# Vision tower with routed experts on one core: softmax scaling on VectorE, biases by matmul, an order of stages for each engine

## What is computed

```python
h = tok(x)                                   # patch projection with shifted images, layer norm
h = h + attn_rope(norm(h))                   # 8 heads, rope; two layer norms; relu net 128-512-128 (x1, net, x2)
h = h + mix(norm(h))                         # triangular W1, gelu, triangular W2, with biases b1, b2
h = h + dif(norm(h))                         # two softmax maps a1 - lam*a2, group norm over features, out_w, out_b
x = norm(h); x1 = ln(x)                      # "moe": attention, then the router
x = x + attn(x1) @ wo
x2 = ln(x)
gate, e = top_2(softmax(x2 @ wr))            # 64 experts, capacity 72 rows each
pos = rank of the (token, choice) in its expert; kept if pos < 72
buf[e, pos] = x2
y = gelu(buf @ w1[e] + b1[e]) @ w2[e] + b2[e]
h = h + x + sum over 2 choices of gate * y[e, pos]
```

## Time and profile before

| what | value |
|---|---|
| median of 3 runs (lowest, highest) | 435.94 us (434.51, 436.28) |
| the profiled execution's own time | 436.75 us |
| its span in the profile | 435.0 us |
| busy: PE / PEld | 311.8 us (72%) / 275.6 us (63%) |
| busy: DVE / ACT / POOL | 229.7 (53%) / 219.0 (50%) / 250.5 us (58%) |
| mean TensorE clock granted | 0.823 of full speed |
| DMA | 50.07 MB |

### The profile page before, as it was taken

How to read it: one execution, slowest core, us unless ns; L and a number is a source line. 1 busy time by engine, 2 the same in 40 slices (tenths; PEclk the granted TensorE clock), 3 DMA queues, 4 the chain that set the end, 5 groups by cost and what they waited for, 6 DMA issues and landing times.

```text
span 435.0 us, 10303 instructions
## 1 busy us (share of the span) xinstructions
PE 311.8 (72%) x3840; PEld 275.6 (63%) x3840; DVE 229.7 (53%) x642; ACT 219.0 (50%) x635; POOL 250.5 (58%) x382
## 2 busy tenths in 40 slices
PE   1886668779775776748785357323999999999960
PEld 0563557677544565736675256212999999999960
DVE  1145585872549999898857763911222323223224
ACT  0133646777478875586676224300255555555530
POOL 5046684778877534374657758778055555555560
PEclk9896869999966977976886558555599999999995
DMA  8999900000000000000000100003888999999406
GB/s 258 425 394 285 124 2 2 3 2 2 1 2 2 2 2 2 3 2 2 2 2 2 27 2 15 6 8 69 159 257 308 306 326 312 324 317 312 163 10 163
DMA packets 25818, 50.07 MB, mean 115 GB/s; under 512 B 4100, under 2 KB 16012, under 8 KB 25642
## 3 DMA queue, kind: packets, MB, share of 16 engines
q1 hardware_dynamic: 22730, 46.91, 35.0%
q0 software_dynamic: 3040, 2.52, 2.0%
HBM read 43.92 MB, written 7.72 MB: 119 GB/s over the span
## 4 chain that ended last, share of the span: by engine, by line
PE 33%; DVE 8%; POOL 4%; ACT 4%; issue 3%; DMA 1%; POOLq 0%; DVEq 0%; SPq 0%
PE bank L705 18%; PE scores L705 13%; ACT work L979 3%; POOL slot_rows L640 2%; DVE work L1207 1%; DVE mx L1197 1%; PE bank L771 1%; PE bank L929 1%; DMA ring<-expert_rows 1%; DVE work L1233 1%; ACT norm L979 1%; DVE norm L1380 1%; DMA expert_rows<-work,put_u 0%; DVE norm L1381 0%; DVE top_i L1299 0%
## 5 line engine op out<-in xcount | busy, mean ns | idle before, releaser
L979 ACT ACTIVATE work<-scores,b1T 128x72 f32<-128x72 f32 x256 | 61.1, 321 | 77.8 <-PE scores L705 77.8
L705 PE MATMUL bank<-ring,work 128*72 128x128 f32 x512 | 98.6, 277 | 0.0
L697 POOL DMA_INDIRECT expert_rows<-work,put_u x64 | 59.9, 936 | 59.7 <-issue 39.5
L705 PE MATMUL scores<-work,ring 128*128 128x72 f32 x512 | 92.2, 265 | 0.0
L705 PEld LDWEIGHTS scores<-work,ring 128*128 128x128 f32 x512 | 80.2, 199 | 0.0
L1369 DVE TENSOR_SCALAR work<-bank,work 72x128 f32<-72x128 f32 x64 | 22.2, 347 | 78.6 <-PE bank L705 78.6
L979 ACT ACTIVATE work<-bank 128x288 f32<-128x288 f32 (+3 forms) x136 | 46.4, 374 | 31.2 <-PE bank L705 25.3
L705 PEld LDWEIGHTS bank<-ring,work 128*72 128x72 f32 x512 | 54.7, 147 | 0.2 <-ACT work L979 0.2
L674 POOL TENSOR_TENSOR work<-work,sm 100x288 f32<-100x288 f32 x32 | 26.0, 834 | 21.3 <-DVE sm L1223 16.4
L979 ACT ACTIVATE work<-work 100x1152 f32<-100x1152 f32 (+1 forms) x20 | 20.4, 1018 | 31.3 <-DVE work L1207 29.6
L705 PE MATMUL bank<-wT,xTp 128*128 128x128 f32 x192 | 33.6, 349 | 1.4 <-ACT work L979 1.4
(11 more groups left out here) (153 smaller groups left out, 614.9 us busy)
## 6 DMA issues: line engine op xcount, KB each, us to landing
ring<-in_experts SPq DMA_DIRECT2D x64, 512.0 KB, 4.9
work<-in_patches SPq DMA_DIRECT2D x4, 864.0 KB, 12.2
slot_rows<-blank SPq DMA_DIRECT2D x1, 2340.0 KB, 30.0
work<-slot_rows SPq DMA_DIRECT2D x7, 292.5 KB
wT<-in_weights SPq DMA_DIRECT2D x1, 1664.0 KB, 17.7
expert_rows<-mid POOLq DMA_DIRECT2D x2, 576.0 KB, 9.3
ring<-expert_rows SPq DMA_DIRECT2D x4, 288.0 KB, 4.6
expert_rows<-work,put_u POOLq DMA_INDIRECT x64, 4.3
```

Of the source, the lines that this page charges most:

```text
L697: pool.indirect_dma_start(out=ytok[:, :], out_offset=bass.IndirectOffsetOnAxis(ap=put_u[:, e:e + 1], axis=0), in_=ys[0:CAP, e % NY, :], in ...
L705: return nc.tensor.matmul(o, a, b, start=start, stop=stop)
L979: return nc.scalar.activation(o, i, f, **kw)
```

## The change

1. The table `ORDER_FOUND` becomes `ORDERS_FOUND` with an own order of the 252 remaining stages for each of the four engines.
2. Softmax scaling: POOL's half (L674) is gone. DVE scales all four quads with one instruction, and `dif_mix` is one instruction instead of four.
3. `mix_base` and `dif_base` are gone. PE puts the bias row into the bank first (`biased`: a matmul with one row of ones, 96 x 384 out), and the output matmuls add to it. The constants grow by 96 columns.
4. `rt_norm_b` on ACT writes straight into `xrow`, without g and b; after `rt_turn` ACT copies the row to its second place (`rows_doubled`). POOL's L627 and L631 are gone. DVE applies g and b per feature when it takes the transposed slot rows to SBUF (`x_in_place`). Since `xrow` has two buffers, ACT waits in `rt_norm_b` of batches 2 and 3 for the scatters of batches 0 and 1.
5. `rt_store` leaves the order: POOL does the four additions after all router stages, before the first expert's scatter.
6. `x1_affine` has two operations instead of three; be1 and b2 are added once.
7. `blank`, the source of the first fill of `slot_rows`, lies in the tile `hid`; ACT waits for that DMA before the first `net_in`.

```diff
-ORDER_FOUND = """
-    tok_z:0 tok_shift:0 tok_z:1 tok_turn:0 tok_norm_a:0 tok_z:2 tok_norm_b:0 tok_shift:1 tok_turn:1 tok_z:3
...
+ORDERS_FOUND = {
+    "pe": """
+    tok_z:0 tok_shift:0 tok_z:1 tok_shift:1 tok_turn:0 tok_z:2 tok_turn:1 tok_shift:2 tok_norm_a:0 tok_z:3
...
-    return [tuple((w.split(":")[0], int(w.split(":")[1]))) for w in ORDER_FOUND.split()]
+    return [tuple((w.split(":")[0], int(w.split(":")[1]))) for w in ORDERS_FOUND[engine].split()]
...
-                if stage in ("mix_base", "dif_base"):
-
-                    pool.wait_ge(S["var"], var_of[name + "_norm_a", b])
-                    pool.tensor_tensor(tiles(mid, b), tiles(h, b), row("L0_ffn_b2" if stage[0] == "m" else "L1_attn_out_b"), ALU.add
-                                       ).then_inc(S["base_ready"], 1)
...
                 if stage == "rt_count":
 
-                    pool.wait_ge(S["normed"], normed_count["rt", b])
                     t = slice(TPB * b, TPB * b + TPB)
-                    st.link(pool.tensor_tensor(tiles(mid, b), tiles(norm, b), row("L1_ffn_ln2_g"), ALU.mult))
                     if b >= 2:
                         pool.wait_ge(slots_sent[b - 2], 16 * 2 * TPB)
-                    st.step(pool.tensor_copy(xrow[:, b % 2, :, :, D], const("ids", TP).rearrange("p (n k) -> p n k", k=2)[:, t, :]))
-                    st.link(pool.tensor_tensor(xrow[:, b % 2, :, :, 0:D], tiles(mid, b).unsqueeze(2).broadcast_to([TP, TPB, 2, D]),
-                                               row("L1_ffn_ln2_b").unsqueeze(2).broadcast_to([TP, TPB, 2, D]), ALU.add))
+                    st.link(pool.tensor_copy(xrow[:, b % 2, :, :, D], const("ids", TP).rearrange("p (n k) -> p n k", k=2)[:, t, :]))
+                    pool.wait_ge(S["rows_doubled"], b + 1)
...
-                if stage in ("rope_sums", "moe_sums", "dif_sums", "dif_sums2"):
...
-                    for q in range(QUADS // 2):
...
-                        last = pool.tensor_tensor(
-                            to, e3, sm[:, s, 2 * PAIRS * q:2 * PAIRS * (q + 1)].unsqueeze(2).broadcast_to([SROWS, 2 * PAIRS, SEQ]), ALU.mult)
...
+            for b in range(NB):
+                pool.wait_ge(S["out_added"], out_count["moe_out", b])
+                pool.tensor_tensor(tiles(h, b), tiles(h, b), tiles(src, b), ALU.add).then_inc(S["h_summed"], 1)
...
+            def biased(job, name):
+
+                o = fill(pe, job)
+                pe.wait_ge(S["rows_in"], 16)
+                mm(o[0:TP, 0:TPB * D], const("ones")[0:1, :], rows[0:1, ROWS.index(name), :].unsqueeze(1).broadcast_to([1, TPB, D]),
+                   start=True, stop=False)
...
+                    if name == "rt" and b >= 2:
+                        act.wait_ge(slots_sent[b - 2], 16 * 2 * TPB)
...
+                    if stage == "rt_turn":
+                        act.wait_ge(S["normed"], normed_count["rt", b])
+                        go(xrow[:, b % 2, :, 1, 0:D], xrow[:, b % 2, :, 0, 0:D]).then_inc(S["rows_doubled"], 1)
...
-                    for q in range(QUADS // 2, QUADS):
...
-                    last.then_inc(S["half_scaled"], 1)
+                    to = e4 if stage[:3] == "dif" else probs[0:SROWS, f % 2, :, :, :, 0:SEQ].rearrange("p q a b k -> p q (a b) k")
+                    v.tensor_tensor(to, e4, s3.unsqueeze(3).broadcast_to([SROWS, QUADS, 2 * PAIRS, SEQ]), ALU.mult
+                                    ).then_inc(S["map_scaled" if stage[:3] == "dif" else "probs_ready"], 1)
...
-                v.tensor_copy(xe[:, e % NX, :], banks[i][:, 0:CAP]).then_inc(S["xe_ready"], 1)
+                v.tensor_scalar(xe[:, e % NX, :], banks[i][:, 0:CAP], col("L1_ffn_ln2_g"), col("L1_ffn_ln2_b"), ALU.mult, ALU.add
+                                ).then_inc(S["xe_ready"], 1)
```

215 lines of the change are left out of this document (142 added, 73 removed).

## The result

The changed kernel took **427.83 us** (median of 4, 427.35 to 428.91), the kernel before 435.23 us beside it (434.21 to 436.28): ratio 0.9836, 95% interval 0.9801 to 0.9871. It is 7.4 us faster. The forecast was 417.4 us in a range from 405 to 430: the sign and the range held, and the gain is 40% of the 18.6 us of the sum. The profiled execution has a span of 425.6 us (before 435.0).

What follows compares the result with a forecast made beforehand. PE alone bounds the experts; before them DVE, POOL and router waits limit stretches. Terms -2 -1 -2 +0.2 -6.0 -7.8 = -18.6 us take the profiled 436.75 to 418.15, median 417.4 us; range 405 to 430 us.

Steps and rivals of the forecast that it cites:

- Biases by matmul: Eight PE bias matmuls, 5.8 us in all, replace POOL additions: 0 on the path, 5.8 us if uncovered; POOL's relief -1 us.
- Up to `dif_out:3` I let both kernels agree: Ahead of the last projection, both kernels were assumed to run alike until `dif_out:3`, in the profile's clock.
- -2 us for DVE's stretch: Between 129.4 and 213 us, where DVE is busy 75.6 of 83.6 us: -2 us, bounds +4 to -6.
- Scaling on DVE: Softmax scaling as one DVE instruction of 1.36 us, POOL's 26.0 us gone; the four `dif_mix` save 1.8 us.
- Start to `dif_scores:1`: From kernel start to DVE's maximum of `dif_scores:1`: -2.8 us forecast.
- To the first expert: Router: -6.0 us to the last projection and -7.8 us from there to the first expert.
- the bound of -10 us: To the last projection: -10 instead of -6.0 us if batch 3's exp did not stand behind `rt_norm_b:2` on ACT.
- Experts: The 64 experts: DVE's longer copies, 8 us more, stay hidden and PE's work is the same: 0.
- More comes free: Rival, 0.14: new orders use DVE's idle time (6 us more), PE gets a higher clock before 305 us (4 us): 407.4 us.
- No effect: Rival, 0.04: the orders lose in new head-of-line waits what POOL gains: 436 us.
- ACT's new waits: Rival, 0.06: `rt_norm_b:3` waits for batch 1's late scatters and stops ACT: 427.4 us.

## Why the prediction was right and wrong

- **Biases by matmul: 0 on the path. Wrong, one of the two steps that failed.** I wrote that these matmuls stand ahead of the wait for the gelu or the group norm, in which PE is idle. For `dif_out` PE came late to its bias row: 1.59 us at 168.39 us without idle time ahead or behind. For `mix_out` it is so in one of four. Measured for `dif_out`: 3.1 us of the middle with the old list (70.65 and 67.50), 4.7 to 6.5 with the own lists (75.64 and 77.47 against 70.96), 5.4 us of the median. The price that I gave "if that cover were gone", 5.8 us, is near it, and belonged into the range of this term. The length was short as well: I took 0.73 us from the mean of one record at mixed clocks, 547 ns, where such a matmul is two records, 0.88 us at a granted clock of 1.00 (209.06 us) and 1.59 us at 0.50 (168.39 us), 8.0 us for the eight and not 5.8.
- **"Up to `dif_out:3` I let both kernels agree", and -2 us for DVE's stretch. Wrong, the other step that failed.** The own lists lose 3.4 us in the middle without the bias rows (70.96 and 67.52) and 5.0 with them (75.64 and 70.65); the medians say 4.9 and some 6. I had +4 as a bound, from the idle time of DVE alone, and read the orders only at the three places of front: all in the router. I never walked the new lists through the stretch which I called DVE's bound. There DVE has 15 us of idle time where it had 7.5.
- **Scaling on DVE: right in size.** 1361 ns and 1356 ns against 1.36 us; alone it moves nothing (1.0005). Of the -1.8 us of DVE's sum the middle shows 0.6 (59.99 to 59.36 us).
- **Start to `dif_scores:1`: right in size**, -2.9 us against -2.8. It is the lists again: with the old one the start is 148.39, so the operations cost 0.8 us and the lists gain 3.7. Both are differences of single executions, which scatter by up to 3 us here, so that the start agrees to 0.1 us is chance.
- **To the first expert, -13.8 us: right in size** (-14.4 and -0.2). The rows follow my steps with everything 3 us late, since the slot numbers of batch 0 came at 242.9 and not at 239.8 us:

```profile
253.08 1.26 ACT L1050 ACTIVATE xrow<-src,rstd 96x128 f32<-96x128 f32 x3 [3.62 <-POOL rstd L648]
256.15 1.15 ACT L1050 ACTIVATE work<-work 100x1152 f32<-100x1152 f32 x1
265.66 0.55 DVE L1328 TENSOR_TENSOR src<-bank,src 96x384 f32<-96x384 f32 x1 [2.11 <-PE bank L765]
270.62 1.05 POOL L716 DMA_INDIRECT slot_rows<-xrow,flat_u  x1 [0.81 <-POOL xrow L707]
281.96 0.97 POOL L716 DMA_INDIRECT slot_rows<-xrow,flat_u  x1 [0.80 <-POOL xrow L707]
295.68 1.95 PE L765 MATMUL scores<-work,ring 128*128 128x72 f32 x8
```

  ACT stands idle for POOL's root, as forecast; the exp starts at 256.15 (252.8 forecast), `moe_out:3` is added by 266.2 (263.5), and the first expert comes 29.5 us later (27.7). Against the earlier trace rows the last step is 6.0 us shorter than before, where I had 7.8. `moe_out:3` is done 3.3 us earlier than before; counted from `moe_sums:1`, which comes 5.2 us later, that is 8.5 us, where I had 6.0. The two misses offset each other. What was wrong in it is the bound of -10 us, the worth of ACT's wait: without the wait nothing is gained (430.07 against 428.99 us).
- **Experts, 0: right.** 129.9 us from the first expert to the end, before and after (425.6 - 295.7, 435.0 - 305.05).
- **Rivals.** *More comes free* did not happen as the change was made. The higher clock that it expects from a PE less idle came in the router alone (PE busy for 59% after 51%, clock 0.73 after 0.62); in the middle PE is less idle too (71% after 68%) and the clock fell (0.73 after 0.78). *No effect*, 436 us, had a mechanism that did: the orders lose in new waits, though only in the middle and only a part of what the rest gains. The chances hold 0.10 for one more case: in DVE's stretch POOL's steps of the root, 0.88 us each, hold up each of 14 long DVE instructions, 12.3 us, which makes 429.7 us. It is near in its number and not the cause: no run shows such a loss, and the scaling alone, with the same long instructions, leaves the middle at 67.49 us. What the trace shows is small and mostly on the other side. Two POOL steps beside a DVE subtraction take 1.30 and 1.45 instead of 0.27 us, 2.2 us of POOL's time in the middle, and end close behind it (164.51 after 164.39 us, 185.25 after 185.12 us); DVE waits 0.17 us behind the second. *ACT's new waits*, 427.4 us, is nearest to the result, by chance: ACT does stand idle for 5.03 us ahead of `rt_norm_b:3`, but for POOL's root, and the slot numbers of batch 3 are still there 2.7 us before their first scatter.

That the result lies in the range is no merit of the middle, which was off by 10.1 us: the range was wide enough for it by its rivals and the bounds of the other terms. A kernel with the bias of `dif_out` on POOL and the old list in the middle, which is what the forecast took for granted there, was run: 418.7 us against 417.4. Its profile has -4.0 us at the start, 0.0 in the middle and -13.8 in the rest, where the sum has -2.8, -2 and -13.8, so a part of this agreement is two misses that offset each other. That version beats both kernels, by 3.9% and 2.1% (0.9612 and 0.9612 / 0.9819 = 0.979), the last from two ratios on the same chip.

## What to carry to other kernels

When a change gives each engine its own order, walk each of the lists through the busiest stretch, not only through the places where it visibly moves work: lists found together could not be mixed here (15 to 25 us lost in the middle), and can be worse than the old one in a part and better in the others, so try them part by part. Work moved "into idle time" of another engine needs a row that shows the idle time at that very place and instance, with the length at the clock granted there (here 1.59 us at 0.50 and 0.88 us at 1.00), and a wait behind it. And before paying for relief on an engine without pauses, look how far behind it the next chain ends: 5 to 7 us off POOL were worth 2 at most, since the slot numbers had only 0 to 1.8 us of slack ahead of their scatters.
